# Routed experts in a transformer layer: dense multiplication replaced by gathered blocks of 64 token slots

## What is computed

```python
scores = sigmoid(x_flat @ gate_weight.T)            # 512 tokens, 32 experts
scores_for_choice = scores + bias
# 2 of 4 groups of 8 experts are kept, then the 4 best experts of those
topk_idx = lax.top_k(masked, 4)[1]
tw = take_along_axis(scores, topk_idx)
tw = tw / (tw.sum(-1) + 1e-20) * 2.5
combine = zeros((512, 32)).at[arange(512)[:, None], topk_idx].add(tw)
# swiglu(x, g, u, d) = silu(x @ g.T) * (x @ u.T) @ d.T, inner width 128
routed = sum over e of combine[:, e] * swiglu(x, w1[e], w3[e], w2[e])
shared = swiglu(x, ws1, ws3, ws2)
return routed + shared
```

## Time and profile before

| | |
|---|---|
| median of 3 runs | 382.76 us (382.57 to 383.10) |
| span of the profiled execution | 380.7 us; no other time of that execution is listed |
| PE / PE weight load busy | 90% / 71% |
| VectorE (DVE) / ScalarE (ACT) / POOL busy | 75% / 50% / 55% |
| mean granted TensorE clock | 0.981 of 2.4 GHz |
| moved by DMA | 32.13 MB, 84 GB/s over the span |

### The profile page before, as it was taken

The page is one execution under the profiler, slowest core; times in us unless marked ns, Lnnn a source line. Parts: engine busy times, 40 slices in busy tenths (PEclk is TensorE's granted clock), DMA queues, the critical chain, the costliest instruction groups (busy, mean ns, idle before and its releaser), DMA issues.

```text
span 380.7 us, 5266 instructions
## 1 busy us (share of the span) xinstructions
PE 340.8 (90%) x1698; PEld 269.7 (71%) x1698; DVE 284.5 (75%) x527; ACT 191.2 (50%) x405; POOL 209.1 (55%) x146
## 2 busy tenths in 40 slices
PE   4767779988989989899798978999999999999996
PEld 3534457765877758676587867778888888888884
DVE  4476664898978989799867966968788887776653
ACT  3425667685777868678545654323323223223222
POOL 0733807880086900969600140038888888888851
PEclk9989999999999999999989997899999999999999
DMA  7900041000500023000420000047554555542001
GB/s 263 385 0 1 2 159 64 0 0 17 206 3 1 2 80 128 2 0 2 127 82 2 0 2 0 2 145 293 164 179 147 162 177 149 169 125 72 13 0 55
DMA packets 14043, 32.13 MB, mean 84 GB/s; under 512 B 1952, under 2 KB 4128, under 8 KB 14016
## 3 DMA queue, kind: packets, MB, share of 16 engines
q1 hardware_dynamic: 14016, 31.79, 25.0%
HBM read 31.20 MB, written 0.59 MB: 83 GB/s over the span
## 4 chain that ended last, share of the span: by engine, by line
PE 29%; POOL 26%; DVE 16%; issue 8%; ACT 6%; DMA 1%; POOLq 1%; ACTq 0%; DVEq 0%
POOL rtmp L957 13%; POOL msplit L946 8%; PE bank L444 6%; PE bank L429 5%; POOL qsp L946 5%; DVE nmax L736 3%; PE bank L406 3%; DVE pT L749 2%; PE bank L384 2%; PE bank L420 2%; PE bank L421 2%; PE bank L331 2%; PE bank L332 2%; PE bank L333 2%; DVE prob L744 1%
## 5 line engine op out<-in xcount | busy, mean ns | idle before, releaser
L253 POOL TENSOR_TENSOR rtmp<-abuf,rope 128x512 f32<-128x512 f32 x22 | 29.2, 1326 | 74.2 <-issue 57.2
L645 ACT ACTIVATE rtmp<-bank 128x512 f32<-128x512 f32 x33 | 19.8, 599 | 83.6 <-PE bank L333 83.6
L946 POOL TENSOR_TENSOR msplit<-wring,msplit 128x768 fp32r<-128x768 f32 x21 | 38.8, 1846 | 39.0 <-DVE msplit L786 38.7
L331 PE MATMUL bank<-xnT,msplit 128*128 128x512 f32 x132 | 54.9, 416 | 3.2 <-DVE msplit L702 1.8
L825 DVE TENSOR_TENSOR pT<-rtmp,pT 128x512 fp32r<-128x512 f32 x33 | 38.3, 1161 | 24.4 <-ACT pT L654 24.3
L736 DVE TENSOR_REDUCE nmax<-bank 128x1 f32<-128x512 f32 x64 | 43.4, 681 | 16.2 <-PE bank L421 15.1
L957 POOL TENSOR_TENSOR rtmp<-rtmp,roped 128x512 f32<-128x512 f32 x30 | 51.3, 1711 | 4.3 <-ACT rtmp L645 4.3
L332 PE MATMUL bank<-xnT,msplit 128*128 128x512 f32 x132 | 52.5, 398 | 0.0
L333 PE MATMUL bank<-xnT,msplit 128*128 128x512 f32 x132 | 52.5, 398 | 0.0
L592 ACT ACTIVATE prob<-bank,nmax 128x512 f32<-128x512 f32 x48 | 33.1, 689 | 32.4 <-DVE nmax L736 31.9
L749 DVE TENSOR_TENSOR pT<-bank,pT 128x512 fp32r<-128x512 f32 x64 | 43.5, 680 | 1.0 <-ACT pT L600 1.0
(11 more groups left out here) (136 smaller groups left out, 685.2 us busy)
## 6 DMA issues: line engine op xcount, KB each, us to landing
wring<-in_w_exp SPq DMA_DIRECT2D x33, 384.0 KB, 4.2
roped<-combine_scratch SPq DMA_DIRECT2D x30, 256.0 KB, 3.5
wring<-in_w_attn SPq DMA_DIRECT2D x16, 224.0 KB, 3.9
wring<-in_w_attn SPq DMA_DIRECT2D x4, 640.0 KB, 7.9
wring<-in_w_attn SPq DMA_DIRECT2D x4, 512.0 KB, 6.8
rope<-in_rope_q SPq DMA_DIRECT2D x1, 768.0 KB, 6.6
x_sb<-in_x SPq DMA_DIRECT2D x1, 512.0 KB, 3.5
out_T<-prob SPq DMA_DIRECT2D x2, 256.0 KB, 2.0
```

Source lines behind the costliest of these rows:

```text
L331: pe.matmul(out_ap, a_hi, b_hi, start=first, stop=False)
L946: pool.tensor_tensor(w_slots[n % SPL][:, 1, :], raw_v[:, n % RAW, :], f(w_slots[n % SPL][:, 0, :]), ALU.subtract).then_inc(wx_lo, 1)
```

## The change

The dense loop over 33 experts is replaced.

The shared expert is multiplied for all tokens in plain float32 before the routed ones, with its weights loaded separately. Its result is added to x on VectorE.

The 2048 pairs are sorted into blocks of 64 slots. Each expert has one static block, for the first 64 tokens sent to it. What is over goes to up to 32 further blocks, each with an expert chosen at run time. PE counts the tokens for each expert and their ranks by matmuls with triangular and all-one matrices (`moe_c`, loaded during attention); VectorE turns the rank into a slot number (`slots`); 32 float32 matmuls invert the list, so that each slot knows its token (`inv_ps`), and `tables` makes from it two lists of row numbers: rows to gather, and rows to scatter to. Empty slots gather some valid row and scatter into rows that nobody reads. `eo` holds the expert of each further block.

Normalised rows are written to DRAM (`xn_dram`). Then 32 units run, unit u with further block u in slots 0 to 63 and static block u in slots 64 to 127:

- POOL gathers 128 rows of 1 KB from `xn_dram` by an indirect transfer (a ring of 6);
- PE transposes them (2 transposes), ScalarE evicts them;
- PE multiplies by both experts' input projections: 4 float32 matmuls of 256 columns with 64 weight columns each; ScalarE silu, VectorE gate;
- PE transposes the result (1), VectorE evicts it, PE multiplies the output projections (2 float32 matmuls of 256 columns), VectorE evicts;
- POOL scatters 128 rows of 1 KB to `y_dram` by an indirect transfer (a ring of 4), without weights.

SP loads two experts' weights, 384 KB each, for each unit: a ring of 10 for the static ones in the former ring, 9 slots for the chosen ones in space of attention, whose number SP reads from SBUF into a register (`value_load`). When all scatters are in, four transfers bring the four expert rows of each token back; VectorE adds them to x with their weights, and x is stored, no longer transposed. The splits of weights and activations, the weighting on POOL and the broadcast of weights through DRAM are gone from this part.

The core of the diff, with eight columns of indentation taken off:

```diff
-RAW = 2 * WGRP // WE
-SPL_M, SPL = 3, 5
-POOL_HI = 5
-AHEAD = 3
+BLK = 64
+NU = E
+WS = 2 * WGRP // WE
+WD_A, WD_R = 2 * (NQT + 1) * T // WE, NPG * NQT * T // WE
+WD = WD_A + WD_R
+XG, XS, YS, GS = 6, 4, 4, 3
...
+    def load_static(e):
+        sp.dma_start(ws_v[:, e % WS, :], w_exp[e]).then_inc(d_ws[e % WS], 16)
+    def load_over(o):
+        e = sp.value_load(eo[0:1, o:o + 1], min_val=0, max_val=E - 1)
+        sp.dma_start(wd_slots[o % WD], w_exp[bass.ds(e, 1), :, :].rearrange("e p n -> (e p) n")) \
+            .then_inc(d_wd[o % WD], 16)
...
+    for tt in range(TT):
+        sp.wait_ge(x2_n, tt + 1)
+        sp.dma_start(xn_dram[tt * P:(tt + 1) * P, :], xn[:, tt, :]).then_inc(d_xn[tt], 16)
+    sp.wait_ge(eo_done, 1)
+    for o in range(WD):
+        load_over(o)
+    for u in range(NU):
+        if u + WD < NU:
+            sp.wait_ge(yu_mm, 2 * u + 2)
+            load_over(u + WD)
+        if u + WS < NU:
+            load_static(u + WS)
+    for r in range(YS):
+        sp.wait_ge(d_yu[r], 16 * (NU // YS))
+    for tt in range(TT):
+        sp.dma_start(y4[:, tt, :, :], y_dram[0:TOPK * T, :].rearrange("(k t p) d -> t p k d", k=TOPK, t=TT)[tt]) \
+            .then_inc(d_y4[tt], 16)
...
-    def expert_in(n):
...
-    def expert_out(n):
...
+    def x_rows(u):
+        pe.wait_ge(d_xg[u % XG], 16 * (u // XG + 1))
+        if u >= 2:
+            pe.wait_ge(xt_ev, u - 1)
         for dc in range(ND):
+            mm = pe.transpose(xt_ps[u % 2][:, dc * P:(dc + 1) * P], xg[:, u % XG, dc * P:(dc + 1) * P], ident[:, :])
+        mm.then_inc(xt_mm, 1)
+    def hidden(u):
+        pe.wait_ge(xt_ev, u + 1)
+        pe.wait_ge(d_wd[u % WD], 16 * (u // WD + 1))
+        pe.wait_ge(d_ws[u % WS], 16 * (u // WS + 1))
+        if u >= 2:
+            pe.wait_ge(gu_done, u - 1)
+        for dc in range(ND):
+            for s, w in enumerate((wd_slots[u % WD], ws_v[:, u % WS, :])):
+                mm = pe.matmul(hu_ps[u % 2][s * BLK:(s + 1) * BLK, 0:2 * I], xTu[:, u % XS, dc, s * BLK:(s + 1) * BLK],
+                               w[:, dc * 2 * I:(dc + 1) * 2 * I], start=(dc == 0), stop=(dc == ND - 1))
+                if dc == ND - 1:
+                    mm.then_inc(hu_mm, 1)
+    def g_rows(u):
+        pe.wait_ge(gu_done, u + 1)
+        if u >= 2:
+            pe.wait_ge(gt_ev, u - 1)
+        pe.transpose(gt_ps[u % 2][:, 0:P], gu[:, u % 2, :], ident[:, :]).then_inc(gt_mm, 1)
+    def out_rows(u):
+        pe.wait_ge(gt_ev, u + 1)
+        if u >= 2:
+            pe.wait_ge(yu_ev, u - 1)
+        for s, w in enumerate((wd_slots[u % WD], ws_v[:, u % WS, :])):
+            pe.matmul(yu_ps[u % 2][s * BLK:(s + 1) * BLK, 0:D], gTu[:, u % GS, s * BLK:(s + 1) * BLK],
+                      w[:, 2 * ND * I:2 * ND * I + D], start=True, stop=True).then_inc(yu_mm, 1)
...
+    pe.wait_ge(d_moe, 16)
+    pe.wait_ge(em_done, 1)
+    for tt in range(TT):
+        mm = pe.matmul(cnt_ps, emask[:, tt, :], ones_e, start=(tt == 0), stop=(tt == TT - 1))
+    mm.then_inc(cnt_mm, 1)
...
+    pe.wait_ge(r_done, 1)
+    for k in range(NK):
+        if k == 0:
+            pe.wait_ge(ov_one, 1)
+            pe.wait_ge(st_done, 1)
+        mv_st = one_st.rearrange("p (t e k) -> p t e k", t=TT, k=TOPK)[:, k // TOPK, :, k % TOPK]
+        for s, one in enumerate((one_ov[:, k * E:(k + 1) * E], mv_st)):
+            mm = pe.matmul(inv_ps[s * BLK:(s + 1) * BLK, :], one_r[:, k, :], one, start=(k == 0), stop=(k == NK - 1))
+            if k == NK - 1:
+                mm.then_inc(inv_mm, 1)
+    pe.wait_ge(sh_sum, TT)
+    for j in range(NU + 3):
+        if j < NU:
+            x_rows(j)
+        if j >= 3:
+            g_rows(j - 3)
+        if 1 <= j <= NU:
+            hidden(j - 1)
+        if j >= 3:
+            out_rows(j - 3)
...
-        gate(0)
...
-        gate_lo(0)
+        dve.tensor_reduce(emask[:, :, :], eq, AX.X, ALU.add).then_inc(em_done, 1)
...
+        dve.wait_ge(cnt_mm, 1)
+        link(dve.tensor_scalar(over[0:E, 0, :], cnt_ps, 1.0 / BLK, -(BLK / 2 + 0.5) / BLK, ALU.mult, ALU.add))
+        link(dve.tensor_scalar(over[0:E, 1, :], over[0:E, 0, :], 8388608.0, None, ALU.add))
+        dve.tensor_scalar(over[0:E, 2, :], over[0:E, 1, :], -8388608.0, 0.0, ALU.add, ALU.max).then_inc(ov_done, 1)
...
+        sel = sel_a.rearrange("p (t e k) -> p t e k", t=TT, k=TOPK)
+        link(dve.tensor_tensor(sel, eq, slotf[:, :, :].unsqueeze(3).to_broadcast([P, TT, E, TOPK]), ALU.mult))
+        link(dve.tensor_reduce(pick[:, :].rearrange("p (t k) -> p t k", t=TT), sel.rearrange("p t e k -> p t k e"),
+                               AX.X, ALU.add))
+        dve.tensor_copy(picki[:, 0, :], pick[:, :])
+        link(dve.scalar_tensor_tensor(vals[:, :], pick[:, :], 4096.0, val_row, ALU.is_ge, ALU.mult))
+        link(dve.tensor_scalar(picki[:, 1, :], picki[:, 0, :], 6, None, ALU.logical_shift_right))
+        link(dve.tensor_copy(pickf[:, 0, :], picki[:, 1, :]))
+        dve.tensor_tensor(one_ov.rearrange("p (i e) -> p i e", e=E), iota_over.unsqueeze(1).to_broadcast([P, NK, E]),
+                          pickf[:, 0, :].unsqueeze(2).to_broadcast([P, NK, E]), ALU.is_equal).then_inc(j_done, 1)
...
+        dve.tensor_tensor(one_r, iota_b.unsqueeze(1).to_broadcast([P, NK, BLK]),
+                          pickf[:, 1, :].unsqueeze(2).to_broadcast([P, NK, BLK]), ALU.is_equal).then_inc(r_done, 1)
+        dve.tensor_tensor(one_st.rearrange("p (t e k) -> p t e k", t=TT, k=TOPK), eq,
+                          vals[:, :].rearrange("p (t k) -> p t k", t=TT).unsqueeze(2).to_broadcast([P, TT, E, TOPK]),
+                          ALU.mult).then_inc(st_done, 1)
+        dve.wait_ge(eo_mm, 1)
+        dve.tensor_scalar(eo[0:E, :], eo_ps, float(E - 1), None, ALU.min).then_inc(eo_done, 1)
...
+        link(dve.scalar_tensor_tensor(found[:, :], inv_ps, 0.0, pad_row, ALU.is_equal, ALU.mult))
+        link(dve.scalar_tensor_tensor(idx[:, 0, :], inv_ps, -1.0, found[:, :], ALU.add, ALU.add))
+        dve.tensor_scalar(idx[:, 1, :], idx[:, 0, :], T - 1, None, ALU.bitwise_and).then_inc(idx_done, 1)
...
+    dve.wait_ge(sh3_mm, 1)
+    dve.wait_ge(sh_silu, 1)
+    dve.tensor_tensor(sh_g, sh_ps[1][:, :], sh_s, ALU.mult).then_inc(sh_gated, 1)
+    slots()
+    top_weights()
+    tables()
+    for tt in range(TT):
+        if tt % 2 == 0:
+            dve.wait_ge(sh_mm, tt // 2 + 1)
+        dve.tensor_tensor(x_sb[:, tt, :], sy_ps[tt // 2][:, (tt % 2) * D:(tt % 2 + 1) * D], x_sb[:, tt, :],
+                          ALU.add).then_inc(sh_sum, 1)
+    for j in range(1, NU + 3):
+        if j >= 3:
+            gT_evict(j - 3)
+        if j <= NU:
+            gated(j - 1)
+        if j >= 3:
+            y_evict(j - 3)
+    dve.wait_ge(sh_sum, TT)
+    for tt in range(TT):
+        dve.wait_ge(d_y4[tt], 16)
+        for k in range(TOPK):
+            last = dve.scalar_tensor_tensor(x_sb[:, tt, :], y4[:, tt, k, :], topw[:, 1, tt, k:k + 1], x_sb[:, tt, :],
+                                            ALU.mult, ALU.add)
+            if k < TOPK - 1:
+                link(last)
+        last.then_inc(fin, 1)
...
+    pool.wait_ge(j_done, 1)
+    one = one_ov.rearrange("p (i e) -> p i e", e=E)
+    pool.tensor_tensor(one, one, val_row.unsqueeze(2).to_broadcast([P, NK, E]), ALU.mult).then_inc(ov_one, 1)
+    def gather(u):
+        if u >= XG:
+            pool.wait_ge(xt_mm, u - XG + 1)
+        pool.indirect_dma_start(xg[:, u % XG, :], None, xn_dram, bass.IndirectOffsetOnAxis(idx[:, 1, u:u + 1], 0)) \
+            .then_inc(d_xg[u % XG], 16)
+    def scatter(u):
+        pool.wait_ge(yu_ev, u + 1)
+        pool.indirect_dma_start(y_dram, bass.IndirectOffsetOnAxis(idx[:, 0, u:u + 1], 0), yu[:, u % YS, :], None) \
+            .then_inc(d_yu[u % YS], 16)
+    for tt in range(TT):
+        pool.wait_ge(d_xn[tt], 16)
+    pool.wait_ge(idx_done, 1)
+    for u in range(XG):
+        gather(u)
+    for u in range(NU):
+        scatter(u)
+        if u + XG < NU:
+            gather(u + XG)
```

More of the change, by code:

```diff
@@ L110, in build @@
         emask = sb("emask", [P, TT, E])
-        esel = sb("esel", [P, TT, E])
+        slotf = sb("slotf", [P, TT, E])
+        ranklo = sb("ranklo", [P, TT, E])
+        pick = sb("pick", [P, NK])
+        picki = sb("picki", [P, 3, NK], U32)
+        pickf = sb("pickf", [P, 2, NK])
+        vals = sb("vals", [P, NK])
+        topw = sb("topw", [P, 2, TT, TOPK])
+        over = sb("over", [P, 3, E])
+        found = sb("found", [P, E])
+        idx = sb("idx", [P, 2, NU], U32)
+        eo = sb("eo", [P, E], U32)
         wsum = sb("wsum", [P, TT, 3])
-        comb = sb("comb", [P, TT, E])
-        combT = prob[0:E, 2, :]
         epsc = sb("epsc", [P, 1])
@@ new lines, in build @@
+        w_shared = gmat[:, :, :, :].rearrange("p j k n -> p (j k n)")
+        xT_f = kvr[:, :, :, :].rearrange("p n a c -> p (n a c)").rearrange("p (d t) -> p d t", d=ND)
+        eq_v = prob[:, 0, :]
+        sh_s, sh_g = prob[:, 1, :], prob[:, 2, :]
+        one_st, one_ov = rtmp[:, 0, :], rtmp[:, 1, :]
```

(54 more changed lines are left out.)

334 lines of the change are left out of this document (123 added, 211 removed).

## The result

The changed kernel takes 391.71 us at the median of 4 runs (388.98 to 395.29), where the kernel before takes 382.93 us (382.57 to 384.09). The ratio is 1.0195, with a 95% interval of 1.013 to 1.026; it leaves out the changed kernel's longest execution, 395.29 us, a slow one. The kernel is slower, by 1.3% at least; 370 us were forecast, and the range of 356 to 404 us holds the result. The profiled execution took 388.98 us, its span 387.2 us, 1.8 us less.

What follows compares the result with a forecast made beforehand. PE and POOL were taken as tied at 4.05 to 4.1 us per expert. Unit 0 leaving PSUM at 278.6, POOL transfers 75.4, then 13.3 to the end gave 367.3; with 2.1 around it, forecast 370 us, range 356 to 404.

Steps and rivals of the forecast that it cites:

- So POOL sets the beat, narrowly.: Unit loop: POOL's gather and scatter, 2.6 us, set the time per unit (the beat), just above PE's 2.1.
- the ramp before unit 0: First gather, before the unit loop: 1.3 us of POOL work plus 2.5 landing, so unit 0 begins at 271.1.
- g: POOL's time for one indirect transfer of 128 rows, in gathers and scatters: taken as 1.3 us.
- Break-even: The transfer time on POOL above which the change loses, all else kept: 1.53 us.
- The rival by POOL (402 us): Unit loop: an indirect transfer costs 1.85 us, from slowing beside VectorE, giving 402 us; chance 0.19.
- The clock rival (393 us): Unit loop: PE at half clock needs 3.55 us a unit and binds; 393 us for half the stage; chance 0.13.
- The DMA rival (384 us): Unit stage: loads and row transfers, 29.6 MB at 322 GB/s, take 92 us, ending at 384; chance 0.12.
- The inversion: Routing, before the first gather: 64 PE records of 32 columns that invert the slot list, taken as 7 us.
- the route's end: Routing, end of emask: moves forward from 245.98 to 244.6 us, as gate and low half, 0.69 each, leave.
- the down projection: Shared expert's, queued on PE ahead of the counts: 8 records at half clock, taken as 3.5 us.
- The large items of `slots()`: VectorE in routing: six items of 512 elements, one of 1024, plus ranklo, found and slotf: 4.9 us.
- The tail from the last scatter to the end of the span: After the last scatter's issue: landing 2.0, expert-row loads 7.0, last four multiply-adds 1.8, store 2.5 us.

Runs made afterwards that it cites:

- e13: The changed kernel run again unedited, on the chip of the order-or-chip comparison: 393.27 us, ratio 1.0309 to the kernel before.
- e14: Changed kernel with gathers issued three steps earlier, ahead of the scatters: 383.54 us, ratio 1.0034 to the kernel before.
- group C: Four follow-up kernels run together on one of four chips, where the kernel before took 381.97 us.
- e17: The program of e10 run again on another chip: 378.74 us.
- e10: Changed kernel with gathers three steps earlier and no weights loaded beyond those that first fill the rings (outputs wrong): 361.54 us, one run.
- e16: The same program as e9 on another chip: 379.85 us, ratio 0.9941 to the kernel before.
- e9: Changed kernel with gathers three steps earlier and the shared down projection moved behind the `eo` matmul: 360.72 us, ratio 0.9408 to the kernel before.
- e5: Changed kernel with gathers three steps earlier, 8 transposed-row and 16 output buffers instead of 4 each: 383.56 us, ratio 1.0058 to the kernel before.
- e6: As e5, with chosen experts' weights loaded for the first nine units only (outputs wrong): 378.65 us, ratio 0.9912 to the kernel before.
- e18: The changed kernel run a third time, unedited, on another chip: 389.64 us, ratio 1.0143 to the kernel before.
- e3: Changed kernel without any weight loads after those that fill the rings (outputs wrong): 381.85 us, one run.

## Why the prediction was wrong

- **The step that failed:** "So POOL sets the beat, narrowly." Its price was right and its place in the queue was not read. The prediction counted a gather's way from issue to landing once, 3.8 us in the ramp before unit 0, and left it out of the loop, as though six buffers were six steps of lead. Behind the scatter they are three. From the first scatter to the last the stage took 95.1 us (370.58 - 275.44) where 74.1 were forecast (2.4 a unit, as the first six gathers were done by then). These 21 us are the miss.
- **How they divide:** 9.7 us are the missing lead (e13 against e14). The late increments of TensorE go with 17 to 19 us in kernels that have the lead, between group C and another for the same program (e17 and e10, e16 and e9), and the weights' bytes with some 5 (e5 against e6). How much either makes in the changed kernel itself isn't shown: of the 95 us of its chain 36.4 are eight landings of gathers, and pauses of more than 0.8 us come to 3.4. The parts overlap, so they aren't added.
- **g was right:** 1.3 forecast, 0.97 to 1.00 us plus a gap of 0.30 measured, 1.28. Break-even stood at 1.53. In group C, with the lead, the forecast's mechanism is what the chain shows, and 360.72 us even lies under 370, in a kernel with two edits that the forecast did not have. Whether the change as it stands would be faster there was not tried; its three-step lead against landings of 5.6 us speaks against it.
- **The rival by POOL (402 us)** did not come: an indirect transfer kept 0.94 to 1.16 us throughout. The rule of the Trainium skill (SBUF — State Buffer, Who interferes with whom) did not strike, as the rows had it: the unit's VectorE operations read PSUM. The rival's own price was misread: 1.28 us in the earlier trace rows is for 512 elements and 1.85 for 768, so the step between them is mostly size and not stretch.
- **The clock rival (393 us)** has nearly the right time for the wrong reason. PE had half the clock in the first units (8 records of L546 in 1.91 us against 1.01), and 0.93 to 1.00 after it, with three transposes in every unit; in other traces of the same kernel it was 0.77 to 0.91 (e13, e18). The chain of the stage ran through the gathers and not through a slow PE.
- **The DMA rival (384 us)** had the rate right: 312 to 323 GB/s at a share of 0.92, against its 322. It had the place wrong: with the weights gone the beat only fell to 2.93 (e3), so the rate costs mostly by lengthening the landings inside the loop.
- **Mis-sized terms.** The inversion took 3.65 us, not 7: 64 records, 0.057 us apart at half clock. The first gather was issued at 259.98 instead of 267.3: 3.4 us by the inversion, 1.4 by the route's end (243.2 against 244.6), 1.5 by the down projection (1.99 against 3.5), 1 by the rest. Unit 0 began at 265.22, 5.2 us later instead of 3.8, and its output needed 10.2 us to the first scatter instead of 7.5, at half the clock: of 7.3 us gained, 3 were left at 275.44. The large items of `slots()` are added wrongly: those named come to 4.2 us, six of 0.7 and one of 1.4 to 5.6, and the sum has 4.9. That the chain has 5.0 for them (0.70, 1.06, 0.69, 1.95 and 0.61) is luck. The columns of PE fall by a factor of 3.1 as written, by six only if the two halves count once. The tail from the last scatter to the end of the span took 16.6 us against 14.6. It begins so:

```profile
370.58 2.41 DMA y_rows<-nmat,idx
373.00 0.03 SPq L368
373.03 0.04 issue
373.07 3.92 DMA ctT<-y_rows
```

After these come 16 multiply-adds of 0.48 us one behind the other, 8 us. The prediction had priced the last four, 1.8 us, as if the loads came one by one; VectorE waited for none after the first. The loads took 3.9 us, not 7.0, which hid half of that miss.

## What to carry to other kernels

A ring of buffers gives no more lead than the queue in which its refill is issued: write down, for each refill, what stands in front of it on its engine and what that waits for, and put the landing inside that loop. Issue the loads of later steps ahead of the stores of earlier ones on the same queue; here that one edit was worth 7 to 10 us of 390, and with the moved projection the kernel is faster than the one before on both chips that ran it, by 6% on one and 0.6% on the other. Compare on one chip: the kernel before moved by 0.3% between the groups, the program with both edits by 5%, and e17 shows that this is not a matter of streaming near the DMA limit. Where a chain says that an engine starts late after nothing, look at when the semaphore rose before the engine is blamed.

## What was unexpected

- An indirect transfer of 128 rows of 1 KB holds GpSimd for 0.97 us (gather) and 0.99 (scatter), and the next starts 0.30 us later at the earliest. The last scatter landed 2.4 us after its issue, with nothing beside it.
- Two matmuls on the two halves of 64 columns start within 0.01 us of each other and cost one: 8 records of 256 columns in 1.01 us.
- In 275 to 345 us of the changed kernel 208 of 5,895 packets on the weights' queue took over three times the median of 0.121 us; in e9 it was 9 of 6,299. The 17 to 19 us between the groups, in a stage of some 70 to 90, came with and without this traffic.
- TensorE's increments came up to 5.6 us after the recorded end of their matmuls (e6), while VectorE's and ScalarE's stood within 0.01 us of theirs, in the same traces.
